# A deformable convolution's last stage: nine taps read where they lie, in 32-by-32 tiles of TensorE, for two row pairs at once

## The chip, the cores and the metric

The kernel runs on one core of a Trainium2 chip. The metric is device time in microseconds of one execution. The kernel before was timed three times; the profile is of one execution, taken by the hardware profiler, in which instructions of TensorE (PE, with its weight loads as PEld), VectorE (DVE), ScalarE (ACT), GpSimd (POOL) and SyncE (SP, which issues all DMAs of the main loop) have their start and duration.

## What is computed

Eight images of 32 channels, 128 by 128, fp32. Two blocks follow each other, each adding its result to its input after a normalization per channel:

```python
x = x + _L0_conv_ref(_gn(x), ...)      # spectral mix in x and y, plus a 1x1 channel mix
x = x + _L1_conv_ref(_gn(x), ...)      # deformable 3x3 convolution
# inside _L1_conv_ref: 27 offset/mask channels by a plain 3x3 convolution,
# nine samples per output pixel at shifted places, bilinear, times a sigmoid mask, then
out = jnp.einsum('bckhw,ock->bohw', vals, weight.reshape(Oc, -1, K2))   # the last stage
return out + bias[None, :, None, None]
```

The change is about the last einsum (nine taps `k`, 32 input channels `c`, 32 output channels `o`), the bias and the residual that is added behind it.

## The kernel before, in words

Four images make a group of 128 partitions (partition = 32 * image + channel); there are two groups. The first block and the second normalization end at about 285 us. Everything after that is the main loop, over 128 row pairs (two groups of 64). A row pair is 2 rows by 128 columns, 256 pixels for each of the 128 partitions.

Every engine runs the same software pipeline, `step(N, q, on, place)` with `q = N % 2`, in six rounds `r`. Step N computes, for different row pairs:

- for pair N: the offsets and masks (`OM`, line 983, round 0; their transposition, line 1005, round 1; then ACT, DVE and POOL make interpolation weights, lines 569 to 589, 739, 576, 579, 493);
- for pair N - 1: in each round POOL and ACT make products and their fp16 halves (lines 469, 559, 478), DVE transposes them (line 718), PE spreads them over the pixels of a region (`expand`, line 950, into the four PSUM banks of `pE`), and ACT and DVE each copy half of `pE` to SBUF (lines 565 and 731). In four of the rounds PE also transposes image strips (line 1016), which ACT copies (line 598);
- for pair N - 2: in each round the samples `V` (line 971), 2 or 3 column tiles times 4 images, into `pV`, copied to `VS[q]` by ACT (line 585), in round 3 by DVE (line 750). Here a partition is 32 * image + channel, and the nine taps lie beside each other in the free dimension;
- for pair N - 3: the last convolution. It contracts over 96 rows = 3 values of ky times 32 channels. For that, SP copies `VS` from one set of partitions to another through twelve DMAs per pair (line 405) into `v2`; in round 4 PE does 12 matmuls (line 996), DVE adds bias and residual `x1r` (line 758), and SP stores `outs` (line 392).

On PE the order within a step is: `expand` of the round, V of the round, then in round 0 OM, in round 4 the convolution, in round 1 the transposition of OM, and in rounds 1, 2, 3 and 5 the strip transposes. An fp32 matmul stands in the trace as two matmul records, each with its weight load; so 12 matmuls are 24 records. A transpose or an fp16 matmul is one record.

In the steps at the start, in the middle and at the end the code is written out (`peeled`); all others are a loop of two steps. The first steps have no convolution yet, since no pair has come so far.

## Time and profile before

| | us |
|---|---|
| median of 3 runs | 2406.02 (2404.01 to 2407.63) |
| the profiled execution, its own time | 2404.01 |
| its span, first to last instruction | 2402.0 |
| main loop, from about | 285 |

How to read it: the page first gives each engine's busy time. A second view, the timeline, shows instructions in the order of time, equal ones merged: start in us, busy us of the merged piece, engine, line, operation, what it writes and reads, its count, and in brackets the idle time of the engine ahead of it with the instruction that ended that. "issue" there is idle time that no other engine ended. A third view cuts the time into windows and gives the clock that was granted to TensorE in them (1.00 is 2.4 GHz, 0.50 is 1.2 GHz).

### The profile page before, as it was taken

To read this page: it belongs to the slowest core of one execution; us is meant where nothing else is said; L and a number is where in the kernel's file an instruction comes from. 1 tells how busy PE (TensorE), PEld (TensorE's weight loads), DVE (VectorE), ACT (ScalarE), POOL (GpSimd) and SP (SyncE) were. 2 spreads that over 40 slices of the span, in tenths; PEclk is the share of its full clock that TensorE was granted. 3 is DMA by queue.
4 is the path that set the end of the run, shared out by engine and by line. 5 is a ranking of instruction groups with operands and counts; after the bars stand their busy time and mean duration, and the time that the engine had idled before them with its cause. 6 is when DMAs were issued, how large, how long until landed. Compare 5 with 4: busy or idle time off the path is not lost.

```text
span 2402.0 us, 126528 instructions
## 1 busy us (share of the span) xinstructions
PE 2034.2 (85%) x50241; PEld 1359.9 (57%) x50241; DVE 1585.7 (66%) x2558; ACT 1787.6 (74%) x3238; POOL 1400.8 (58%) x1803
## 2 busy tenths in 40 slices
PE   8555188988988998898998899889889888988985
PEld 3311056666666666666666666666666666666663
DVE  8699066666666666666666666666666666666663
ACT  0003488888888888888888888888888888888884
POOL 0000166666666666666666666666666666666662
PEclk9699599999999999999999999999999999999997
DMA  8036545556555555655555555565555556556553
GB/s 311 1 140 271 200 115 154 147 149 156 143 149 150 147 151 148 156 143 150 152 147 151 151 154 147 148 156 144 148 152 146 150 148 155 145 149 154 145 151 87
DMA packets 196541, 363.81 MB, mean 151 GB/s; under 512 B 39760, under 2 KB 122480, under 8 KB 192368
## 3 DMA queue, kind: packets, MB, share of 16 engines
q1 hardware_dynamic: 196464, 362.74, 55.7%
q8 instruction: 54, 0.88, 0.2%
q14 instruction: 23, 0.19, 0.0%
HBM read 159.38 MB, written 52.22 MB: 88 GB/s over the span
## 4 chain that ended last, share of the span: by engine, by line
PE 29%; ACT 21%; issue 21%; SPq 5%; DVE 5%; POOL 2%; ACTq 1%; DVEq 1%; DMA 0%; POOLq 0%
PE pV L971 8%; PE pM L996 8%; ACT halves L559 7%; ACT big L585 5%; PE pE L950 5%; SPq L405 4%; PE pR L1016 4%; ACT big L576 4%; PE pM L983 4%; ACT big L598 3%; DVE big L731 2%; DVE big L718 1%; ACT msk L589 1%; POOL halves L478 1%; POOL prod L469 1%
## 5 line engine op out<-in xcount | busy, mean ns | idle before, releaser
L478 POOL TENSOR_TENSOR halves<-prod,halves 128x300 f16<-128x300 f32 x768 | 626.4, 816 | 377.2 <-ACT halves L559 377.1
L731 DVE COPY big<-pE 128x768 f32<-128x768 f32 x768 | 716.9, 933 | 191.3 <-PE pE L950 189.0
L971 PE MATMUL pV<-big 128*32 128x144 f32 x16384 | 816.9, 331 | 4.7 <-issue 1.4
L565 ACT ACTIVATE big<-pE 128x768 f32<-128x768 f32 x768 | 659.7, 859 | 107.7 <-PE pE L950 107.6
L469 POOL TENSOR_TENSOR prod<-big 128x300 f32<-128x300 f32 x768 | 554.2, 722 | 100.8 <-POOL big L493 32.2
L718 DVE STREAM_TRANSPOSE big<-halves 128x384 f32<-128x384 f32 x768 | 440.2, 573 | 197.2 <-POOL halves L478 193.4
L950 PE MATMUL pE<-big,sel_s 32*128 32x64 f16 (+1 forms) x24576 | 411.3, 203 | 174.8 <-DVE big L731 103.6
L950 PEld LDWEIGHTS pE<-big,sel_s 32*128 32x128 f16 x24576 | 329.6, 92 | 386.0 <-issue 373.4
L971 PEld LDWEIGHTS pV<-big 128*32 128x32 f32 x16384 | 482.2, 112 | 102.2 <-issue 6.7
L559 ACT ACTIVATE halves<-prod 128x300 f16<-128x300 f32 x768 | 484.3, 631 | 3.2 <-POOL prod L469 3.0
L493 POOL TENSOR_TENSOR big<-big,msk 128x360 f32<-128x360 f32 x128 | 107.2, 838 | 484.5 <-ACT big L579 484.5
L1016 PE MATMUL pR<-ident,strips 128*128 128x128 f32 x2048 | 330.2, 284 | 38.6 <-ACT big L598 38.6
L585 ACT ACTIVATE big<-pV 128x432 f32<-128x432 f32 (+1 forms) x640 | 315.0, 492 | 12.5 <-PE pV L971 12.5
L598 ACT ACTIVATE big<-pR 128x512 f32<-128x512 f32 x512 | 307.2, 600 | 20.1 <-PE pR L1016 3.1
L1016 PEld LDWEIGHTS pR<-ident,strips 128*128 128x128 f32 x2048 | 221.8, 141 | 161.5 <-ACT big L598 85.0
L739 DVE TENSOR_TENSOR big<-pM,cols_s 128x720 f32<-128x720 f32 x128 | 116.4, 909 | 219.6 <-ACT msk L589 219.6
L983 PE MATMUL pM<-big,wom 96*32 96x256 f32 x3072 | 193.7, 384 | 47.1 <-DMA big<-xh_scratch 47.1
L569 ACT ACTIVATE om_s<-pM,bom_s 128x256 f32<-128x256 f32 x128 | 61.4, 479 | 213.7 <-PE pM L983 213.7
L996 PE MATMUL pM<-v,wc 96*32 96x256 f32 x3072 | 203.7, 395 | 14.2 <-DMA v<-big 14.2
L983 PEld LDWEIGHTS pM<-big,wom 96*32 96x32 f32 x3072 | 99.8, 112 | 103.1 <-issue 50.6
L758 DVE SCALAR_TENSOR_TENSOR outs<-pM,bias_s,x1r 128x256 f32<-128x256 f32 x128 | 62.6, 489 | 128.8 <-PE pM L996 128.8
L996 PEld LDWEIGHTS pM<-v,wc 96*32 96x32 f32 x3072 | 103.5, 111 | 72.5 <-DMA v<-big 15.4
(72 smaller groups left out, 1175.1 us busy)
## 6 DMA issues: line engine op xcount, KB each, us to landing
v<-big SPq DMA_DIRECT2D x1536, 96.0 KB
win<-xh_scratch SPq DMA_DIRECT2D x128, 544.0 KB, 4.2
big<-xh_scratch SPq DMA_DIRECT2D x384, 136.0 KB, 4.1
xh_scratch<-win SPq DMA_DIRECT2D x32, 544.0 KB, 2.7
big<-in_x SPq DMA_DIRECT2D x16, 1024.0 KB, 16.4
x_scratch<-big SPq DMA_DIRECT2D x16, 1024.0 KB, 3.9
x1r<-x_scratch SPq DMA_DIRECT2D x128, 128.0 KB, 2.1
out<-outs SPq DMA_DIRECT2D x128, 128.0 KB, 1.8
```

Source lines behind the costliest of these rows:

```text
L469: nc.gpsimd.tensor_tensor(prod[:, rn % 2, :, :].rearrange("p m (a b) -> p m a b", a=NSH), hy.to_broadcast([P, RB, NSH, NSH]), hx.to_broadc ...
L478: nc.gpsimd.tensor_tensor(half[:, rn % 2, :, 0:SQ, 1], prod[:, rn % 2, :, :], half[:, rn % 2, :, 0:SQ, 0], ALU.subtract).then_inc(low_done, 1)
L559: nc.scalar.activation(half[:, rn % 2, :, 0:SQ, 0], prod[:, rn % 2, :, :], ACT.Copy).then_inc(high_done, 1)
L565: nc.scalar.activation(*expanded(1 - q, r, 0), ACT.Copy).then_inc(e_act, 1)
L585: nc.scalar.activation(*evacuate(q, r), ACT.Copy).then_inc(v_act, 1)
L718: nc.vector.transpose(PT[:, rn % 2, :], halves[:, rn % 2, :]) \
L731: nc.vector.tensor_copy(*expanded(1 - q, r, 1)).then_inc(e_dve, 1)
L950: last = mm(o, sel_s[part, (i + ky) * (KS + 1) + ox, :], rhs, start=(h == 0), stop=(h == 1))
L971: last = mm(pV[r % 2][b * C:(b + 1) * C, o:o + TAPC], XT[q][:, t * P + b * C:t * P + (b + 1) * C], av[:, b * NT + t, :, :], start=True, st ...
L983: last = mm(pM[b * C:(b + 1) * C, 0:PX], wom[:, kx, :], wino[0:KS * C, q, b, :, x0:x0 + W], start=(kx == 0), stop=(kx == KS - 1))
L996: last = mm(pM[b * C:(b + 1) * C, PX:2 * PX] .rearrange("p (i t j) -> p t i j", i=TILE_R, t=NT), wc[:, kx, :], v2[:, b, :, :].rearrange("p ...
L1016: last = nc.tensor.transpose(pR[:, u * P:(u + 1) * P], strips[:, t:t + 2, :, :].rearrange("p s r x -> p (s r x)"), ident[:, :])
```

## The change

The convolution is done once in two steps, at the head of every even step (`q == 0`, round 0), for the pairs N - 4 and N - 3, which lie in `VS[0]` and `VS[1]`. It reads `VS` in place: each matmul contracts over the 32 channels of one image, for one tap. There are 16 outputs, 4 images times 4 rows (2 pairs of 2 rows), each 32 output channels by 128 columns, in 16 different 32-by-32 tiles of the array (row of the tile from the image, column from the output row). Each output accumulates ten matmuls: nine taps, and one with the identity that brings the residual. So 160 matmuls (320 records with as many weight loads) for two pairs stand where 24 matmuls (48 records) stood. The results go to columns 384 to 511 of the four banks of `pE`. ACT copies two of the banks with the bias, DVE the other two. The twelve copies per pair between partitions, `v2` and DVE's line 758 are gone. The samples' layout in `VS` and in `pV` has all nine taps apart (`k=TAPS`), so the V matmul writes its output in runs of two elements.

```diff
-        wc = sb("wc", [KS * C, KS, C])
-        v2 = sb("v2", [KS * C, IPG, KS, PX])
+        wc = sb("wc", [P, TAPS, C])
...
+        pC = pE[:, :].rearrange("p (a n) -> p a n", a=QUADS)[:, :, RPX:RPX + W]
...
-            dst = VS[q].rearrange("p (k t n) -> p t k n", k=KS, t=NT)[:, tiles[0]:tiles[0] + n]
-            return dst, pV[gi % 2][:, 0:n * TAPC].rearrange("p (t k n) -> p t k n", t=n, k=KS)
+            dst = VS[q].rearrange("p (k t n) -> p t k n", k=TAPS, t=NT)[:, tiles[0]:tiles[0] + n]
+            return dst, pV[gi % 2][:, 0:n * TAPC].rearrange("p (t k n) -> p t k n", t=n, k=TAPS)
...
+                sp.dma_start(wc[r, :, :], wct.rearrange("k c o -> c k o")).then_inc(blocks_ld, 16)
...
-                if on[3]:
+                if on[3] and q == 0:
+                    g, local = place(N - 4)
+                    sp.wait_ge(out_act, N - 2)
+                    sp.wait_ge(out_dve, N - 2)
+                    rows = out[g * P:(g + 1) * P, bass.ds(local * PX, 2 * PX)] \
+                        .rearrange("(b o) (r x) -> r o b x", b=IPG, x=W)
+                    for k in range(2 * TILE_R):
+                        sp.dma_start(rows[k], outs[k * C:(k + 1) * C, :, :]).then_inc(out_st, 16)
+                if on[2] and q == 1:
                     g, local = place(N - 3)
-                    for b in range(IPG):
-                        for ky in range(KS):
-                            sp.dma_start(v2[ky * C:(ky + 1) * C, b, :, :].rearrange("c k n -> c (k n)"),
-                                         VS[q][b * C:(b + 1) * C, ky * KS * PX:(ky + 1) * KS * PX]) \
-                                .then_inc(v2_ld, 16)
+                    wait(sp, conv_done, N - 3)
+                    sp.dma_start(x1r[:, :], x1_d[g * P:(g + 1) * P, bass.ds(local * PX, 2 * PX)]).then_inc(x1_ld, 16)
...
+                    if on[3] and q == 0 and r == 0:
+                        act.wait_ge(conv_done, N - 2)
+                        wait(act, out_st, (N - 4) * 32)
+                        nc.scalar.activation(outs[:, 0:2, :], pC[:, 0:2, :], ACT.Identity,
+                                             bias=bias_s[:, 0:1]).then_inc(out_act, 2)
...
+                    if on[3] and q == 0 and r == 0:
+                        dve.wait_ge(conv_done, N - 2)
+                        wait(dve, out_st, (N - 4) * 32)
+                        nc.vector.tensor_scalar(outs[:, 2:4, :], pC[:, 2:4, :], bias_s[:, 0:1], None,
+                                                ALU.add).then_inc(out_dve, 2)
...
-                    if on[3] and r == CONV_AT:
-                        n = N - 3
-                        dve.wait_ge(conv_done, n + 1)
...
-                        nc.vector.scalar_tensor_tensor(out=outs[:, 1 - q, :], in0=pM[:, PX:2 * PX],
-                                                       scalar=bias_s[:, 0:1], in1=x1r[:, 1 - q, :],
-                                                       op0=ALU.add, op1=ALU.add).then_inc(out_ready, 1)
...
+                    if on[3] and q == 0 and r == 0:
+                        pe.wait_ge(e_act, min(N - 1, PAIRS) * ROUNDS if isinstance(N, int) else (N - 1) * ROUNDS)
+                        pe.wait_ge(e_dve, min(N - 1, PAIRS) * ROUNDS if isinstance(N, int) else (N - 1) * ROUNDS)
+                        pe.wait_ge(v_act, (N - 2) * VN[1])
+                        pe.wait_ge(v_dve, (N - 2) * VN[0])
+                        pe.wait_ge(x1_ld, N * 8 - 16)
...
+                        for k in range(TAPS + 1):
+                            kx, ky = divmod(k, KS)
+                            for b, d, i in itertools.product(range(IPG), range(2), range(TILE_R)):
+                                c, row = slice(b * C, (b + 1) * C), d * TILE_R + i
+                                if k < TAPS:
+                                    w, rhs = wc[c, ky * KS + kx, :], VS[d][c, k * PX:(k + 1) * PX] \
+                                        .rearrange("p (t i x) -> p i t x", t=NT, i=TILE_R)[:, i]
+                                else:
+                                    w, rhs = ident[c, c], x1r[c, row * W:(row + 1) * W].rearrange("p (t x) -> p t x", t=NT)
+                                last = mm(pC[row * C:(row + 1) * C, b, :].rearrange("p (t x) -> p t x", t=NT), w, rhs,
+                                          start=(k == 0), stop=(k == TAPS))
+                        last.then_inc(conv_done, 2)
                     if on[1]:
+                        if on[3] and q == 0 and r == 1:
+                            pe.wait_ge(out_act, N - 2)
+                            pe.wait_ge(out_dve, N - 2)
                         expand(N - 1, r)
...
-                                last = mm(pV[r % 2][b * C:(b + 1) * C, o:o + TAPC],
+                                last = mm(pV[r % 2][b * C:(b + 1) * C, o:o + TAPC]
+                                          .rearrange("p (k m j) -> p m k j", k=KS, j=2),
                                           XT[q][:, t * P + b * C:t * P + (b + 1) * C],
-                                          av[:, b * NT + t, :, :], start=True, stop=True)
+                                          av[:, b * NT + t, :, :, :], start=True, stop=True)
...
-                    if on[3] and r == CONV_AT:
-                        n = N - 3
-                        pe.wait_ge(v2_ld, (n + 1) * (16 * NV2))
...
-                        for kx in range(KS):
-                            for b in range(IPG):
-                                last = mm(pM[b * C:(b + 1) * C, PX:2 * PX]
-                                          .rearrange("p (i t j) -> p t i j", i=TILE_R, t=NT), wc[:, kx, :],
-                                          v2[:, b, :, :].rearrange("p k n -> p (k n)")
-                                          .rearrange("p (m k j) -> p m k j", k=KS, j=2)[:, :, kx, :],
-                                          start=(kx == 0), stop=(kx == KS - 1))
-                        last.then_inc(conv_done, 1)
```

## Rows read from the trace of the kernel before

**Rows 1.** The page's first part: engine, busy us, share of span, instructions
```profile
PE 2034.2 (85%) x50241; PEld 1359.9 (57%) x50241; DVE 1585.7 (66%) x2558; ACT 1787.6 (74%) x3238; POOL 1400.8 (58%) x1803
```
**Rows 2.** Windows: us, busy per engine (count), granted clock, DMA share, GB/s
```profile
1295.00:1425.00 130.00, 117.00 (x3103) 81.12 (x3096) 85.72 (x128) 108.31 (x200) 86.27 (x111) 1.00 0.60 154
1100.00:1230.00 130.00, 117.03 (x3108) 80.38 (x3107) 86.71 (x129) 109.39 (x202) 87.82 (x113) 1.00 0.58 151
```
**Rows 3.** Timeline of one step of the loop, from round 4 to OM
```profile
1214.09 0.53 PE L950 MATMUL pE<-big,sel_s 32*128 32x64 f16 x32 [0.50 <-issue]
1215.21 1.58 PE L996 MATMUL pM<-v,wc 96*32 96x256 f32 x24
1215.24 0.92 DVE L731 COPY big<-pE 128x768 f32<-128x768 f32 x1
1216.71 0.53 PE L950 MATMUL pE<-big,sel_s 32*128 32x64 f16 x32
1217.00 0.48 DVE L758 SCALAR_TENSOR_TENSOR outs<-pM,bias_s,x1r 128x256 f32<-128x256 f32 x1 [0.84 <-PE pM L996]
1217.96 0.66 PE L1016 MATMUL pR<-ident,strips 128*128 128x128 f32 x4
1218.09 0.41 ACT L585 ACTIVATE big<-pV 128x288 f32<-128x288 f32 x1
1218.96 0.54 PE L950 MATMUL pE<-big,sel_s 32*128 32x64 f16 x32 [0.35 <-DVE big L731]
1219.51 1.17 PE L971 MATMUL pV<-big 128*32 128x144 f32 x24
1220.50 1.48 PE L983 MATMUL pM<-big,wom 96*32 96x256 f32 x24
1221.91 0.53 PE L950 MATMUL pE<-big,sel_s 32*128 32x64 f16 x32
1222.13 0.48 ACT L569 ACTIVATE om_s<-pM,bom_s 128x256 f32<-128x256 f32 x1 [1.60 <-PE pM L983]
```
**Rows 4.** Timeline, PE alone, of an early step that has no convolution
```profile
323.94 0.54 PE L950 MATMUL pE<-big,sel_s 32*128 32x64 f16 x32 [0.51 <-issue]
...
326.05 0.54 PE L950 MATMUL pE<-big,sel_s 32*128 32x64 f16 x32 [0.80 <-DVE big L731]
...
327.29 0.66 PE L1016 MATMUL pR<-ident,strips 128*128 128x128 f32 x4
...
328.84 1.17 PE L971 MATMUL pV<-big 128*32 128x144 f32 x24 [0.43 <-ACT big L598]
329.79 1.52 PE L983 MATMUL pM<-big,wom 96*32 96x256 f32 x24
```
**Rows 5.** Groups by line: shapes, count, busy us, mean ns of one record, idle before
```profile
L950 PE MATMUL pE<-big,sel_s 32*128 32x64 f16 (+1 forms) x24576 | 411.3, 203 | 174.8 <-DVE big L731 103.6 <-issue 62.8 <-DVE big L718 7.6
L983 PE MATMUL pM<-big,wom 96*32 96x256 f32 x3072 | 193.7, 384 | 47.1 <-DMA big<-xh_scratch 47.1
L996 PE MATMUL pM<-v,wc 96*32 96x256 f32 x3072 | 203.7, 395 | 14.2 <-DMA v<-big 14.2
```
**Rows 6.** DMA queues, window 1290 to 1430, then window 500 to 1290: packets, MB, share
```profile
q8 instruction: 24, 0.39, 1.2%
...
q8 instruction: 1, 0.02, 0.0%
```
**Rows 7.** Timeline of the end of the span
```profile
2374.50 0.41 ACT L585 ACTIVATE big<-pV 128x288 f32<-128x288 f32 x1 [1.08 <-PE pV L971]
...
2382.71 7.74 SPq L405 DMA_DIRECT2D v<-big  x12
2392.09 2.79 PE L996 MATMUL pM<-v,wc 96*32 96x256 f32 x24 [9.88 <-DMA v<-big]
...
2394.95 0.48 DVE L758 SCALAR_TENSOR_TENSOR outs<-pM,bias_s,x1r 128x256 f32<-128x256 f32 x1 [13.14 <-PE pM L996]
```

More of the change, by code:

```diff
@@ L47 @@
 TAPC = TAPS * TILE_R * TILE_C
-OM_AT, OMT_AT, CONV_AT = 0, 1, 4
+OM_AT, OMT_AT = 0, 1
 T_AT = (1, 2, 3, 5)
@@ L224, in build @@
         wino_ld = [sem(f"wino_ld{i}") for i in range(2)]
-        v2_ld = sem("v2_ld")
-        x1_ld = [sem(f"x1_ld{i}") for i in range(2)]
-        out_st = [sem(f"out_st{i}") for i in range(2)]
+        x1_ld = sem("x1_ld")
+        out_st = sem("out_st")
         om_done = sem("om_done")
@@ L388, in step @@
                     load_window(N + 1, 1 - q, place)
-                if on[3]:
-                    g, local = place(N - 3)
-                    sp.wait_ge(out_ready, N - 2)
-                    sp.dma_start(out[g * P:(g + 1) * P, bass.ds(local * PX, PX)], outs[:, 1 - q, :]) \
-                        .then_inc(out_st[1 - q], 16)
-                if on[1]:
-                    g, local = place(N - 1)
-                    wait(sp, out_ready, N - 2)
-                    sp.dma_start(x1r[:, 1 - q, :], x1_d[g * P:(g + 1) * P, bass.ds(local * PX, PX)]) \
-                        .then_inc(x1_ld[1 - q], 16)
-                if on[2]:
-                    sp.wait_ge(v_act, (N - 1) * VN[1])
-                    sp.wait_ge(v_dve, (N - 1) * VN[0])
-                    wait(sp, conv_done, N - 2)
-                    for b in range(IPG):
-                        for ky in range(KS):
-                            sp.dma_start(v2[ky * C:(ky + 1) * C, b, :, :].rearrange("c k n -> c (k n)"),
-                                         VS[q][b * C:(b + 1) * C, ky * KS * PX:(ky + 1) * KS * PX]) \
-                                .then_inc(v2_ld, 16)
+                if on[3] and q == 0:
[7 more added lines that the diff above has]
+                if on[2] and q == 1:
+                    g, local = place(N - 3)
+                    wait(sp, conv_done, N - 3)
+                    sp.dma_start(x1r[:, :], x1_d[g * P:(g + 1) * P, bass.ds(local * PX, 2 * PX)]).then_inc(x1_ld, 16)
             steps(sp, step)
-            for q in range(2):
-                sp.wait_ge(out_st[q], 16 * (NPAIR // 2) * g_count)
+            sp.wait_ge(out_st, 64 * (NPAIR // 2) * g_count)
             sp.wait_ge(flag_set, 1)
@@ L582, in step @@
                         act.wait_ge(v_done, (N - 2) * len(VGROUPS) + (r + 1))
-                        if v_count(1, r) == 0:
-                            wait(act, v2_ld, (N - 3) * (16 * NV2))
+                        if v_count(1, r) == 0 and q == 0:
+                            wait(act, conv_done, N - 2)
                         nc.scalar.activation(*evacuate(q, r), ACT.Copy).then_inc(v_act, 1)
@@ L747, in step @@
                         dve.wait_ge(v_done, (N - 2) * len(VGROUPS) + (r + 1))
-                        if v_count(0, r) == 0:
-                            wait(dve, v2_ld, (N - 3) * (16 * NV2))
+                        if v_count(0, r) == 0 and q == 0:
+                            wait(dve, conv_done, N - 2)
                         nc.vector.tensor_copy(*evacuate(q, r)).then_inc(v_dve, 1)
-                    if on[3] and r == CONV_AT:
-                        n = N - 3
-                        dve.wait_ge(conv_done, n + 1)
-                        dve.wait_ge(x1_ld[1 - q], (n - (1 - q)) * 8 + 16)
-                        m = (n - (1 - q)) * 8
-                        if not (isinstance(m, int) and m == 0):
-                            dve.wait_ge(out_st[1 - q], m)
-                        nc.vector.scalar_tensor_tensor(out=outs[:, 1 - q, :], in0=pM[:, PX:2 * PX],
-                                                       scalar=bias_s[:, 0:1], in1=x1r[:, 1 - q, :],
-                                                       op0=ALU.add, op1=ALU.add).then_inc(out_ready, 1)
             steps(dve, step)
@@ L977, in step @@
                         wait(pe, msk_done, N)
-                        wait(pe, out_ready, N - 3)
                         pe.wait_ge(wino_ld[q], (N - q) * (8 * KS) + 16 * KS)
```

23 lines of the change are left out of this document (11 added, 12 removed).

## The prediction

> **What bounds the kernel now.** I read the page's busy times first [rows 1]: PE is busy for 85% of the span, ACT for 74%, DVE for 66%. In the main loop PE is busy for 117.0 of 130 us at a granted clock of 1.00, the full 2.4 GHz [rows 2]. So PE is nearly the bound, but no engine is full, and what a piece of work is worth must be read from the order of one step. I took the timeline of a step [rows 3], where the reader is to follow PE: E4 (`expand` of round 4) starts at 1214.09, the convolution at 1215.21, E5 at 1216.71, strip transposes at 1217.96, E0 at 1218.96, V0 at 1219.51, OM at 1220.50. From OM a chain of offsets, masks and weights runs through ACT, DVE and POOL to E4 and E5 of the same step, with ACT nearly without a gap. From E4 to the next OM is 6.41 us, and the time of a step is the chain from OM to E4 plus these 6.41. There were 8 steps in 130 us, 16.2 us each [rows 2].
>
> The trace has one stretch of the same six pieces without a convolution, in an early step [rows 4]: E4 at 323.94, E5 at 326.05, OM at 329.79, so 5.85 us. It is the best witness of what removing the convolution brings: 0.56 us, not the 1.50 us that PE gives it. The reader is to see why: E5 there waits 0.80 us for DVE's copy (line 731), which before lay under the convolution (it runs from 1215.24 to 1216.16 in rows 3), and V0 waits 0.43 us for ACT.
>
> **Part by part.**
>
> *Removed, each step:* 24 records on PE, 1.50 us, and DVE's line 758, 0.48 us with its wait of 0.84 us [rows 3]. By the early step both together are worth 0.56 us of a step [rows 3, 4]. The twelve copies per pair end no wait in the loop: the row of the old convolution has no idle time ahead of it [rows 3], and of its 14.2 us of waiting for the copies [rows 5] 9.88 stand ahead of the very last convolution [rows 7]. I price them at nothing in the loop.
>
> *Added, every second step:* 320 records on PE at the head of the step, between the transposes and E0. Call their time T. The trace has no 32-by-32 fp32 tiles running beside each other, so I bound T.
> - Below: OM is six rounds of four tiles, 256 columns; (1.48 - 0.38) / 5 = 0.22 us a round [rows 3, 5], 0.11 us for 128 columns. If all 16 tiles run together there are 20 rounds, 2.2 us.
> - From V: 24 records in 1220.50 - 1219.51 = 0.99 us, six rounds of 0.165 us for 144 columns [rows 3]. Four tiles with weights of their own do not get below this. 20 rounds make 3.3 us.
> - From `expand`, the only piece with 32-row tiles beside each other: (0.53 - 0.20) / 31 = 10.6 ns per record [rows 3, 5]. 320 records make 3.4 us. For 2.2 us a record would have to follow every 6.9 ns, which no row here shows over a whole piece.
> - Above: if only two tile rows of the four run together, 6.6 us; one after the other, 13.2 us (4 x 3.3). `expand` has four tile rows at once, so I give these little.
>
> I take 3.3 us, since two rows of different kind meet there.
>
> The Trainium skill, TensorE: Matmul & The Clock Gate, section "The mechanism", says that tiles of a packed group start about 4 ns apart and then run together; by that rule T would be the lower bound, 2.2 us, and this is the first rival below. No row here shows 4 ns.
>
> *What waits behind it.* The convolution stands ahead of E0 and waits for both copies of E5 and for the last V copy. In the early step the copy of E5 by DVE starts with the end of E5; in rows 3 the last V copy by ACT ends at 1218.50, 1.79 us after E5, the latest of them. So it starts 1.85 us after E5. Then T, 0.1 us to drain (OM: 1221.91 - 1220.50 = 1.41 = 6 x 0.22 + 0.09), about 0.5 us from E0 to V0 and 0.97 us to OM. E4 to OM: 2.11 + 1.85 + T + 0.1 + 0.5 + 0.97 = T + 5.53, against 6.41. Behind the waiting PE stands everything: E0, V0, OM and the chain.
>
> *Sum for two steps:* even step T - 0.88, odd step -0.56, together T - 1.44. With T = 3.3 it is +1.86 us. There are 62 such couples (N = 4 to 126): +115 us.
>
> *Moved to ACT and DVE, every second step:* one copy of 256 elements each, like line 569 (0.48 us) and line 758 (0.48 us). They stand behind the first copies of `expand`, while PE does V0 and OM: E1 comes 2.95 us after E0, ACT's first copy and this one are through after about 0.6 + 0.9 (as line 731) + 0.5 = 2.0 us, and ACT then still waits for OM (1.60 us idle in rows 3). Nothing. If V0 and OM were shorter by 1 us it would cost 0.1 us.
>
> *Access patterns.* V now writes PSUM in runs of two. The nearest row is the old convolution (runs of two read, of eight written) against OM, same columns: 1.50 against 1.41 us, 7% per round [rows 3]. On 32 rounds of 0.165 us that would be 0.37 us a step, +46 us over 126 steps; below, nothing. V reads in runs of two already and gets only 144 columns into 0.165 us, so there is room for the writes: I take 0. The Trainium skill, PSUM — Partial Sum Buffer, section "Specifications (TRN2)", says that any non-contiguous pattern slows matmuls significantly and gives no figure; it speaks for the upper end. The V copies of ACT and DVE write in runs of 16 elements instead of 48; 0.
>
> *SP:* twelve DMA issues fewer per pair, four stores of half the size instead of two, one load instead of two, each with a step of slack: 0. *Start:* the weights of the convolution are loaded in more, smaller pieces, under the second group's image load: 0.
>
> *End of the span.* Before, the last V copy but one ends at 2374.91, then come the copies (7.74 us of issue), a convolution at half clock (2.79 us) and line 758 at 2394.95 [rows 7]. Now the last V group and its copy follow at once (about 1.0 us), then T: 2374.9 + 1.0 + 3.3 = 2379.2, the rest as before. That is -15.8; the convolution at N = 128 costs T - 0.3 = +3.0. Together -13 us.
>
> Span 2402.0 + 115 - 13 = 2504, and 2 us around it (2404.01 against 2402.0) make **2506**. The profiled execution lies 2 us under the median; I leave that.
>
> **The rivals.**
>
> *The tiles run fully together* (T = 2.2). Two steps cost 0.76 us: +47, end -14: 2402 + 33 + 2 = 2437. For it: OM's rounds show no loss with four tiles. Against: V's rounds do. 0.24.
>
> *Something slows PE further.* (a) V's output pattern, +46 us on 2506: 2552. (b) Two tile rows at a time: T = 6.6, 62 x 5.16 = 320, end -10: 2714. (c) Code. In the 8 written-out steps 24 packets of instructions arrive, in 790 us of loop one [rows 6]; so the loop of two steps, some six packets, stays on the chip. It grows from 1552 to 2096 matmul and load records, over eight packets. Should it no longer fit, the fetches come in each turn. The written-out steps, with busy PE 117.00 against 117.03 us, say that costs nothing [rows 2]. But the convolution eats 2.5 packets in 3.3 us, and a packet takes 1.1 us (1.2% of 16 engines over 140 us, over 24); if each is waited for, +2.75 us, 62 times: 2676. The Trainium skill, Advanced Engine Details and Errata, section "ISA Cache", gives TensorE 128 KB, which the new loop would pass and the old one not. Together 0.20 beyond the forecast's own bounds.
>
> *Faster: the freed time comes back whole.* The early step is one step, with pipelines just filling; if the chain of other engines follows PE, removing gives g = 1.5 us per step instead of 0.56. Two steps then cost T - 0.32 - 2g. With T = 2.2: -1.12 x 62 - 14: 2321. With T = 3.3: 2390. It is faster from g = 0.83 (T = 2.2) or g = 1.39 (T = 3.3) upwards. Against: the 0.80 us wait for DVE ahead of E5. 0.10.
>
> *The change does not do what it says:* the tiles serialize altogether, T = 13.2: 62 x 11.76 = 729, end -3: 3130. 0.03.
>
> **How the numbers follow.** The forecast (T from 2.9 to 3.9 us, with up to half of the pattern's cost) has 0.43 and reaches from 2480 to 2565. The range reaches down to the fast tiles and up into the slowed cases: 2430 to 2640; outside are the faster case (0.10) and about 0.09 above. A measurement of this kernel can tell about 0.2% from no change. Faster 0.10, within 0.2% 0.02, slower 0.88.
>
> **What would show it.** The 320 records as one piece of 3.3 us between transposes and E0 of every second step, PE idle about 0.8 us before E5 on DVE, odd steps near 15.6 us and even ones near 18.6 us, V0 to OM still at 0.99 us; ACT idle under the convolution; the end 13 us shorter. Wrong it is if the piece takes 2.2 or over 4 us, if V0 to OM grows, if instruction packets come in the loop, or if odd steps shrink by over 1 us.

## The result, and the profile after

| | before | after |
|---|---|---|
| median of the runs, us | 2405.02 (2399.09 to 2407.63) | 3315.62 (3311.06 to 3317.82) |
| span of the profiled execution, us | 2402.0 | 3311.2 |
| granted clock, mean | 0.97 | 0.83 |
| packets of instructions | 54 | 630 |

The ratio is 1.379 (1.376 to 1.382). I had said 2506, in a range up to 2640. The direction was right; the size was about nine times too small.

The page of the kernel after, first the busy times as in [rows 1], then its queue of instruction packets (packets, MB, share), then three groups of its fifth part (count | busy, mean ns | idle before, releaser):

```profile
PE 2463.6 (74%) x67649; PEld 1662.3 (50%) x67649; DVE 1564.5 (47%) x2494; ACT 1812.7 (55%) x3302; POOL 1387.4 (42%) x1803
...
q8 instruction: 630, 10.32, 1.3%
...
L727 DVE COPY big<-pE 128x768 f32<-128x768 f32 x768 | 718.1, 935 | 1167.7 <-PE pE L941 1166.7
...
L556 ACT ACTIVATE big<-pE 128x768 f32<-128x768 f32 x768 | 648.7, 845 | 919.1 <-PE pE L941 918.8
...
L964 PE MATMUL pE<-big,wc 32*32 32x128 f32 x18432 | 419.2, 396 | 371.9 <-issue 371.4
```

The reader is to see four things. ACT and DVE do as much as before, and their copies of `pE` wait some 900 to 1200 us for PE (108 and 191 us before). PE's own share fell from 85% to 74%, so PE is not full of work either. And ahead of the new convolution (line 964) PE stood idle for 371 us with "issue" as the releaser: no semaphore that the profile shows held it. And there are 12 times as many packets of instructions.

The step times below are the distances between ACT's copies of OM, one for each step. Before they are 16.1 to 16.3 us in both loops. After, the odd steps take 15.6 to 16.3 (median 16.1 in the first loop, 15.6 in the second). The even ones take 30 to 33 in the loops (median 31.4 and 32.1) and 27.0 to 29.2 in the written-out steps between them and in the first turn of the second loop.

The timeline of PE in an even step of the loop, with E0, V0, OM and E1 of it, and ahead of it V0 and OM of the odd step:

```profile
1601.49 1.17 PE L986 MATMUL pV<-big 128*32 128x144 f32 x24 [0.30 <-ACT big L594]
1602.48 1.48 PE L998 MATMUL pM<-big,wom 96*32 96x256 f32 x24
...
1614.42 0.53 PE L941 MATMUL pE<-big,sel_s 32*128 32x64 f16 x32 [0.74 <-DVE big L727]
...
1615.66 0.66 PE L1016 MATMUL pR<-ident,strips 128*128 128x128 f32 x4
1620.16 2.05 PE L964 MATMUL pE<-big,wc 32*32 32x128 f32 x83 [3.84 <-issue]
1622.64 2.81 PE L964 MATMUL pE<-big,wc 32*32 32x128 f32 x128 [0.44 <-issue]
1626.93 1.79 PE L964 MATMUL pE<-big,wc 32*32 32x128 f32 x73 [1.49 <-issue]
...
1629.52 0.61 PE L941 MATMUL pE<-big,sel_s 32*128 32x64 f16 x18
...
1630.91 1.67 PE L986 MATMUL pV<-big 128*32 128x144 f32 x24
1632.35 2.79 PE L998 MATMUL pM<-big,wom 96*32 96x256 f32 x24
1635.07 0.83 PE L941 MATMUL pE<-big,sel_s 32*128 32x64 f16 x32
```

The same in a written-out even step, between the two loops:

```profile
1755.71 0.66 PE L1016 MATMUL pR<-ident,strips 128*128 128x128 f32 x4
1756.46 1.82 PE L964 MATMUL pE<-big,wc 32*32 32x128 f32 x120
1760.33 1.90 PE L964 MATMUL pE<-big,wc 32*32 32x128 f32 x128 [2.04 <-issue]
1765.45 1.11 PE L964 MATMUL pE<-big,wc 32*32 32x128 f32 x37 [3.21 <-issue]
...
1767.35 0.83 PE L941 MATMUL pE<-big,sel_s 32*128 32x64 f16 x32
```

The pieces are the key. The convolution breaks into runs, and a whole run is 128 matmuls with 128 weight loads. A packet has 10.32 MB / 630 = 16.4 KB; over the 256 instructions of a whole run that is 64 bytes each. That these packets are PE's own code can be seen in [rows 6]: 24 came there for eight steps of new code, and eight steps have 4 x 1552 = 6208 matmul and load records of PE, 24.3 packets. So each run is one packet of code: PE eats one in 1.9 us, and the next run starts 5.1 us after it (1760.33 to 1765.45). In the written-out step nothing waits ahead of the first run; in the loop there are 3.84 us more in front of it.

How many packets come, in both stretches of the kernel after (windows as in [rows 2], then the queue in the same window):

```profile
500.00:1600.00 1100.00, 851.85 (x24344) 588.34 (x24334) 494.49 (x725) 646.58 (x1192) 504.44 (x654) 0.83 0.21 55
...
q8 instruction: 232, 3.80, 1.5%
...
1744.00:1874.00 130.00, 102.32 (x3148) 71.95 (x3144) 64.20 (x93) 82.56 (x153) 64.86 (x85) 0.89 0.23 61
...
q8 instruction: 25, 0.41, 1.3%
```

Written out: 130 / 25 = 5.2 us for a packet. In the loop: 1100 / 232 = 4.7 us. Both are averages over stretches in which PE waits for code only part of the time. Two steps have 2096 matmul and load records, 8.2 packets, and took 43.3 us on average where they are written out. That 8.2 x 5.2 gives nearly the same is bookkeeping, since written-out code is fetched once; it doesn't show a limit. The odd step has 2.8 packets, one per 5.5 us, and does not wait. The limit shows where PE stands: within the convolution the trace has the packets 3.3 to 5.7 us apart, in the middle 3.9, while each carries 1.9 us of work. In the loop a turn takes 47.6 us, 10.0 packets, about two more than it holds.

### The profile page after: what moved, and what is told of

It reads as the page before. It is cut to its first block and busy times, and to the rows that moved or that the text cites. A ratio compares the mean times of both kernels' runs of the same rounds, so it can differ in the third digit from the quotient of the medians.

```text
span 3311.2 us, 159684 instructions
## 1 busy us (share of the span) xinstructions
PE 2463.6 (74%) x67649; PEld 1662.3 (50%) x67649; DVE 1564.5 (47%) x2494; ACT 1812.7 (55%) x3302; POOL 1387.4 (42%) x1803
## 3 DMA queue, kind: packets, MB, share of 16 engines
q8 instruction: 630, 10.32, 1.3%
## 5 line engine op out<-in xcount | busy, mean ns | idle before, releaser
L469 POOL TENSOR_TENSOR halves<-prod,halves 128x300 f16<-128x300 f32 x768 | 611.7, 797 | 1312.2 <-ACT halves L550 1312.1
L986 PE MATMUL pV<-big 128*32 128x144 f32 x16384 | 856.3, 342 | 23.2 <-ACT big L594 20.0
L964 PE MATMUL pE<-big,wc 32*32 32x128 f32 x18432 | 419.2, 396 | 371.9 <-issue 371.4
L941 PE MATMUL pE<-big,sel_s 32*128 32x64 f16 (+1 forms) x24576 | 454.0, 211 | 250.5 <-DVE big L727 159.3
L941 PEld LDWEIGHTS pE<-big,sel_s 32*128 32x128 f16 x24576 | 357.4, 96 | 485.7 <-issue 296.7
L986 PEld LDWEIGHTS pV<-big 128*32 128x32 f32 x16384 | 501.2, 117 | 136.5 <-issue 34.9
L964 PEld LDWEIGHTS pE<-big,wc 32*32 32x32 f32 x18432 | 306.4, 131 | 471.3 <-issue 438.8
L594 ACT ACTIVATE big<-pR 128x512 f32<-128x512 f32 x512 | 307.2, 600 | 27.4 <-PE pR L1016 10.3
L581 ACT ACTIVATE big<-pV 128x432 f32<-128x432 f32 (+1 forms) x640 | 310.0, 484 | 11.4 <-PE pV L986 10.9
L998 PE MATMUL pM<-big,wom 96*32 96x256 f32 x3072 | 258.7, 484 | 46.7 <-DMA big<-xh_scratch 46.7
L998 PEld LDWEIGHTS pM<-big,wom 96*32 96x32 f32 x3072 | 122.2, 140 | 135.2 <-issue 99.8
L476 POOL COPY strips<-win 128x1088 f32<-128x1088 f32 x128 | 139.5, 1090 | 0.0
## 6 DMA issues: line engine op xcount, KB each, us to landing
big<-in_x SPq DMA_DIRECT2D x16, 1024.0 KB, 16.3
```

Source lines behind the costliest of these rows:

```text
L469: nc.gpsimd.tensor_tensor(half[:, rn % 2, :, 0:SQ, 1], prod[:, rn % 2, :, :], half[:, rn % 2, :, 0:SQ, 0], ALU.subtract).then_inc(low_done, 1)
L581: nc.scalar.activation(*evacuate(q, r), ACT.Copy).then_inc(v_act, 1)
L941: last = mm(o, sel_s[part, (i + ky) * (KS + 1) + ox, :], rhs, start=(h == 0), stop=(h == 1))
L964: last = mm(pC[row * C:(row + 1) * C, b, :].rearrange("p (t x) -> p t x", t=NT), w, rhs, start=(k == 0), stop=(k == TAPS))
L986: last = mm(pV[r % 2][b * C:(b + 1) * C, o:o + TAPC] .rearrange("p (k m j) -> p m k j", k=KS, j=2), XT[q][:, t * P + b * C:t * P + (b + 1) ...
L998: last = mm(pM[b * C:(b + 1) * C, 0:PX], wom[:, kx, :], wino[0:KS * C, q, b, :, x0:x0 + W], start=(kx == 0), stop=(kx == KS - 1))
```

## The experiments

**Theory A**: the loop's code no longer stays on the chip, and PE waits for it, once behind each jump back and again within the convolution. **Theory B**: the work itself is slow (16 small tiles, weight loads, patterns). Where an expectation has further theories, it names them.

### The kernel before with a loop of four steps

```diff
-UNROLL = 2
+UNROLL = 4
```

> The kernel before with its main loop made four steps long instead of two; every engine does the same work in the same order, only the loop's body is twice as long (about 3100 matmul and weight-load records of TensorE against 1552). Theory A (code): a body that does not fit on the chip is fetched anew in each turn. Then q8 shows some 12 packets per turn, about 3 per step, in the whole loop. The written-out steps of before took 16.2 us with 3 packets per step, so this should cost little in this kernel: 0 to 3%, 2405 to 2480 us. Theory B (the 16-tile piece itself is slow, code plays no part): the same time, and it would also be so under A if fetches at 3 packets per 16 us are always early; the packets tell whether the body is held.

Measured: 2650.9 us, ratio 1.103 (1.101 to 1.105), with 456 packets. The body is fetched in each turn, as Theory A said, but at 10% instead of 0 to 3%: the expectation had priced code by the written-out steps again and left out the jump. The old convolution, no small tile in it. One step of four, the one behind the jump, takes 23 to 24 us (median of each loop), the others mostly 16.2 to 17.5. Its queue from 700 to 1200 us, and PE behind a jump:

```profile
q8 instruction: 97, 1.59, 1.4%
```

```profile
847.59 0.66 PE L1016 MATMUL pR<-ident,strips 128*128 128x128 f32 x4
851.04 0.53 PE L950 MATMUL pE<-big,sel_s 32*128 32x64 f16 x32 [2.79 <-issue]
851.61 1.34 PE L971 MATMUL pV<-big 128*32 128x144 f32 x24
852.71 0.63 PE L983 MATMUL pM<-big,wom 96*32 96x256 f32 x1
853.82 2.78 PE L983 MATMUL pM<-big,wom 96*32 96x256 f32 x23 [0.48 <-issue]
```

What follows: a body that is not held costs 7 to 8 us behind the jump even in the old kernel, by waiting 2.8 us behind the jump, by more waits after it, and by the clock, since OM takes 2.78 us instead of 1.48. A packet comes every 500 / 97 = 5.2 us. A turn of 73 us takes 14 of them and holds 3104 / 256 = 12.1; again about two too many. What the two are, whether code fetched past the jump and thrown away, no row tells. The three steps without a jump ask for a packet per 5.4 us and cost 0 to 1.3 us more than 16.2: that is code just fast enough.

### The kernel after with fewer blocks in the convolution

```diff
-                        for k in range(TAPS + 1):
+                        for k in (*range(3), TAPS):
```

> The changed kernel with the convolution cut to taps 0, 1 and 2 and the residual: 4 of its 10 blocks of 16 matmuls (the other six taps are left out of the output). Records of TensorE in the loop's body: 1712 against 2096. Theory A (code, the body fits on the chip): no instruction packets in the loop, even steps of about 16.2 - 0.88 + 0.4 x 3.3 = 16.6 us, odd ones 15.6, in all about 2385 us. Theory B (16 tiles are slow in themselves, 13 us for ten blocks): the piece takes 4 x 1.3 = 5.2 us, even steps 20.5 us, about 2630 us.

> The changed kernel with 7 of the 10 blocks (taps 0 to 5 and the residual; three taps are left out of the output). Records in the loop's body: 1904. Theory A (code): the edge lies between 1552 records, which are held, and 2096, which are not. If 1904 fit, even steps take 16.2 - 0.88 + 0.7 x 3.3 = 17.6 us, 2450 us in all; if they do not, over 22 us and over 2700 us, with packets in the loop. Theory B: 7 x 1.3 = 9.1 us, even steps 24.4 us, about 2880 us, and on a straight line between 4 and 10 blocks.

The run with seven blocks has `range(6)` in that place.

Measured: 2814.2 us with four blocks (436 packets), 3119.5 with seven (590 packets). Neither theory had 2814: with four blocks the body was expected to stay on the chip, and it did so in part alone. With seven, the even steps take 28.5 in the loop and 24.2 to 25.8 written out. With four, in the first loop they alternate between 17.7 and 25; in the second all take about 26; written out 18.9 to 20.8. Odd steps take 15.6 to 16.3 in both, with two exceptions among the written-out ones of four blocks (18.8 and 16.7). The couples N = 64 to 69 (two of them written out, the third a first turn) had no jump ahead: on average 36.1 us for 6.7 packets, 40.7 for 7.4, and 43.3 for the 8.2 of the kernel after. The time of two steps rises with the number of their instructions, by 4.6 and 2.7 us for equal additions, so not as a fixed price for each. Where four blocks left the even step its 17.7 us, two packets came in it, and five in the one of 25.

### The expansion halved, so that the whole convolution fits

```diff
-                    for h, u in itertools.product(range(2), range(QUADS)):
+                    for h, u in itertools.product(range(1), range(QUADS)):
-                        last = mm(o, sel_s[...], rhs, start=(h == 0), stop=(h == 1))
+                        last = mm(o, sel_s[...], rhs, start=True, stop=True)
```

> The changed kernel with all 10 blocks of the convolution, but with the spreading matmuls (expand) of the high fp16 halves alone: 192 matmuls and as many loads fewer in the loop's body, 1712 records, as many as with 4 blocks. The low halves are left out, so the samples are less exact. Theory A (code): no packets in the loop, the convolution in 3 to 4 us at the full clock, even steps about 18 us; in all 2450 to 2520 us, less what the shorter expand gives. Theory B: the convolution still takes 13 us, over 3200 us.

> The kernel before with the spreading matmuls of the high fp16 halves alone (the low halves are left out, as in a_half_expand). It is the partner of a_half_expand, in whose first group the loop ran without instruction packets at 17.6 + 19.9 = 37.5 us for two steps. Theory A (even with its code on the chip the new convolution costs more than the two old ones, since its piece takes 4.3 us there): 15.3 to 16.0 us a step, 31 to 32 us for two, so the new form is 5 to 6 us slower per couple. Rival (only code is to blame): 18.7 us a step, 37.5 for two.

Measured: the kernel after 2868.7 us with 202 packets, where 2450 to 2520 was expected since the body was to be held throughout; the kernel before 2358.1, with steps of 15.7 and 16.0 as expected. The body has 1712 records with its 320 for the convolution. In the first loop it is held from the twelfth step on; the queue from 500 to 1250 us:

```profile
q8 instruction: 1, 0.02, 0.0%
```

There the steps take 19.9 and 17.6 us, 37.5 for two, where the kernel before with the same cut takes 31.7. In the second loop nearly every other turn has most of the packets and takes 15.4 + 31.2; the one after it has few and takes 15.4 + 19.9. It is the same code and the same work in one execution, so 11.3 us of an even step are the fetching of code, with the clock that falls while PE waits. For these 11.3 us the comparison leaves no room for Theory B: small tiles, patterns and order are the same in both turns. What the held couple costs over the 31.7 of before, 5.8 us, is the work's own. PE of a held stretch, the even step and then the end of the odd one:

```profile
663.81 3.87 PE L964 MATMUL pE<-big,wc 32*32 32x128 f32 x281 [0.49 <-issue]
...
668.13 0.35 PE L941 MATMUL pE<-big,sel_s 32*128 32x64 f16 x16
668.56 1.17 PE L986 MATMUL pV<-big 128*32 128x144 f32 x24
...
681.57 0.51 PE L941 MATMUL pE<-big,sel_s 32*128 32x64 f16 x16 [1.16 <-DVE big L727]
...
685.00 1.67 PE L986 MATMUL pV<-big 128*32 128x144 f32 x24 [0.32 <-ACT big L594]
686.44 2.32 PE L998 MATMUL pM<-big,wom 96*32 96x256 f32 x24
```

The convolution is one run now, 668.13 - 663.81 = 4.32 us, 13.5 ns a record, with the code at hand and V0 at its full-clock 1.17 us. That is T of the prediction, and it is 4.3, not 3.3. In the odd step the granted clock falls near 681.3, after 6 us in which PE was busy for 3.74: E5 0.51 us instead of 0.36, V0 1.67, OM 2.32.

### The loop turned by one step

```diff
-            peeled(0, 4)
+            peeled(0, 5)
-                first, loops = g * NPAIR + 4, (NPAIR - 5) // UNROLL
+                first, loops = g * NPAIR + 5, (NPAIR - 6) // UNROLL
-                        step(j * UNROLL + (first + q), q % 2, [True] * 4,
+                        step(j * UNROLL + (first + q), (q + 1) % 2, [True] * 4,
```

> The changed kernel with its loop turned by one step: the body begins with the odd step, so the jump back falls between an even and an odd step and no longer right ahead of the convolution. All work and its order are the same. Theory A (two costs of code: a wait behind each jump back, 7 us in b_loop4, and packets eaten faster than they come within the convolution): the 3.8 us of idle time ahead of the convolution go, even steps fall from 31.5 to about 27 us, as in the written-out steps, and odd ones rise from 15.6 to 20 to 23 us; in all about the same, 3250 to 3450 us. Rival (the wait ahead of the convolution is a drain or a semaphore of its own): even steps stay at 31.5, odd ones at 15.6.

Measured: 3405.0 us. The jump now stands ahead of the odd step, which takes 22.7 us in the first loop and 20.5 in the second (medians) instead of 16.1 and 15.6; the even one takes 27.4 to 27.6 (26.5 to 28.9) instead of 31.4 to 32.1, as the written-out even steps of the kernel after. The odd step behind the jump:

```profile
1627.40 0.66 PE L1016 MATMUL pR<-ident,strips 128*128 128x128 f32 x4
1631.88 0.56 PE L941 MATMUL pE<-big,sel_s 32*128 32x64 f16 x32 [3.83 <-issue]
1634.74 1.67 PE L986 MATMUL pV<-big 128*32 128x144 f32 x24 [2.30 <-issue]
```

The 3.84 us ahead of the convolution moved with the jump, to work that has nothing to do with it. So the two costs are apart: 4 to 5 us behind a jump that stands ahead of the even step (4.8 to 6.5 ahead of the odd one), and the wait within the convolution.

### The kernel after with a loop of four steps

The edit is that of the first experiment.

> The changed kernel with four steps written out in its loop instead of two, so that half as many jumps back are taken; every operation of the step is the same. Theory A (a turn pays once for the jump, about 4 to 5 us of wait ahead of the convolution, and each convolution pays by itself about 11 us because its instructions come too slowly): the even step behind a jump stays at 31 to 32 us, the other even step of the turn costs what the written-out steps of the changed kernel cost, 27 to 28 us; with some 28 fewer jumps at 4.3 us the time falls by about 120 us, to 3190 (3150 to 3240). Theory B (the surplus is the work itself: small tiles, their order, the output pattern): where the jumps are changes nothing, 3300 to 3330. Theory C (a body of twice the size is worse in every step): over 3330.

Measured: 3196.5 us (Theory A had 3190), 575 packets. Even steps 31 behind the jump, the others 27 to 29, odd ones 15.6 to 16.3. Half the jumps are gone, and the steps without a jump ahead take what the written-out ones take. The same edit costs the kernel before 10% and brings the kernel after 4%: once the code isn't held anyway, a longer body has fewer turns to pay for.

### What a held record costs

All three runs here have the halved expansion too, so that there are stretches whose code is held.

```diff
-                            for b, d, i in itertools.product(range(IPG), range(2), range(TILE_R)):
+                            for d, i, b in itertools.product(range(2), range(TILE_R), range(IPG)):
```

> a_half_expand with the 16 matmuls of a block in another order: image (tile row) fastest, so that neighbours in the queue lie in different tile rows; before it was output row (tile column) fastest. Theory A (the 13.5 ns per record come from starts in one tile row that follow each other): in the stretches whose code is held the piece falls from 4.3 us towards 3.4 us, 10.6 ns per record. Rival (the array or the queue is full at that rate whatever the order): 4.2 to 4.4 us. Slower than 4.4 us would say that alternating rows hurts.

Measured: 2882.1 us; the piece takes 4.33 us, the steps 17.6 and 19.9. Which tile follows which makes no difference.

```diff
-    w, rhs = wc[c, ky * KS + kx, :], VS[d][c, k * PX:(k + 1) * PX] \
-        .rearrange("p (t i x) -> p i t x", t=NT, i=TILE_R)[:, i]
+    w, rhs = wc[c, ky * KS + kx, :], VS[d][c, k * PX + i * W:k * PX + (i + 1) * W] \
+        .rearrange("p (t x) -> p t x", t=NT)
```

> The changed kernel with the expansion from the high halves alone, as in a_half_expand, and with the convolution's samples read as 128 elements in a row instead of 16 runs of 8 (each matmul then reads other samples than the convolution wants; count, shapes and tiles of the matmuls are the same). It tells whether the 4.3 us of the held convolution (13.5 ns for each of 320 records, against the 10.6 ns of my sum) come from reading in runs of 8. If so: the piece takes 3.3 to 3.6 us where the code is held, and the time falls by some 0.8 us in each of about 40 held couples and more where the clock then holds, 2790 to 2850. If not: the piece stays at 4.2 to 4.4 us, its steps at 17.6 and 19.9 us, the time at 2860 to 2890.

Measured: 2866.1 us, 3.87 us for the same 281 records, steps of 17.6 and 19.9. Reading in runs of eight costs nothing here.

```diff
+    t = slice(0, NT // 2) if 0 < k < TAPS else slice(0, NT)
-    last = mm(pC[row * C:(row + 1) * C, b, :].rearrange("p (t x) -> p t x", t=NT), w, rhs,
+    last = mm(pC[row * C:(row + 1) * C, b, :].rearrange("p (t x) -> p t x", t=NT)[:, t], w, rhs[:, t],
```

> The changed kernel with the expansion from the high halves alone, as in a_half_expand, and in the convolution the eight taps 1 to 8 take 64 of their 128 columns (the other half of their sums is left out); tap 0 and the residual keep all 128, so the piece still has 320 matmuls with a weight load each, but 16384 columns by 16 tiles fall to 64 x 128 + 256 x 64. It tells what the 13.5 ns per record of the held convolution are made of. If columns (the tiles share the array's time by columns): 4.3 us fall to 4.3 x 0.6 = 2.6 us, even held steps to about 18.3 us. If each matmul with its load has a floor of its own (an issue or load cost near 10.6 to 13.5 ns): the piece stays at 3.4 to 4.3 us, held steps at 19.0 to 19.9. The steps without held code, 26 to 31 us, are the same in both, since they wait for as many instructions.

Measured: 2844.0 us. A held even step, PE alone:

```profile
492.25 3.07 PE L965 MATMUL pE<-big,wc 32*32 32x128 f32 x284 [0.53 <-issue]
...
495.73 0.35 PE L941 MATMUL pE<-big,sel_s 32*128 32x64 f16 x16
...
497.13 1.49 PE L999 MATMUL pM<-big,wom 96*32 96x256 f32 x24
```

The piece takes 495.73 - 492.25 = 3.48 us, 0.84 less than 4.32, for 256 halved records: 3.3 ns each, from 13.5 to 10.2 ns (which takes the other 64 as unchanged). Columns alone would have given 6.8. So both views held in part. A record of 64 columns costs 10.2 ns, close to the 10.6 ns of `expand`, whose records have 64 columns too; one of 128 costs 13.5. My sum had put the price of a 64-column record on one of 128. The held steps were mostly 15.4 and 19.1 us, 34.5 together: 3.0 less than in a_half_expand, of which 0.84 is the piece and 2.2 the odd step, where the clock did not fall.

### Versions of the kernel before

The timeline showed [rows 3] that E5's copy by DVE can wait behind line 758 and that E4 to E5 hangs on the convolution between them. I moved line 758 a round later, and a third of the convolution (kx of 0) a round earlier:

```diff
-                    if on[3] and r == CONV_AT:
+                    if on[3] and r == ROUNDS - 1:
                         n = N - 3
                         dve.wait_ge(conv_done, n + 1)
...
-                    if on[3] and r == CONV_AT:
+                    if on[3] and r in (CONV_AT - 1, CONV_AT):
...
-                        for kx in range(KS):
+                        for kx in (range(1) if r < CONV_AT else range(1, KS)):
...
-                        last.then_inc(conv_done, 1)
+                        if r == CONV_AT:
+                            last.then_inc(conv_done, 1)
```

The other three versions take one part of this edit or shift it, as their expectations say.

> The kernel before with its old convolution in two parts: the four matmuls of kx = 0 in round 3 behind V, where TensorE then waits for ACT, the eight of kx = 1 and 2 in round 4 as before, and DVE's line 758 in round 5 behind its copy of expand instead of ahead of its transpose. Same work in all. Theory (what the convolution costs is what does not fit under DVE's copy ahead of E5, 0.56 us a step by the early step): 0.2 to 0.45 us a step come back, 126 times, 2350 to 2385 us. Rival (the chain through ACT sets the step, V0 waits for it anyway): under 0.1 us a step, 2395 to 2406 us.

> The kernel before with one edit: VectorE's addition of the convolution's result (its line 758) is done one round later, and the convolution stays whole where it was. In b_split this was done together with moving a third of the convolution a round earlier, and its steps took 15.7 us instead of 16.2, yet its written-out stretches took 18 to 20 us, with 8.6 us of waits for V's transfers ahead of the convolution in 90 us. If the gain came from VectorE (E's copy of the next round had waited behind the addition): steps of 15.8 to 16.0, written-out stretches as before, 2360 to 2392. If it came from the split: within 0.3% of the kernel before, 2398 to 2412.

> The kernel before with two thirds of the convolution (kx of 0 and 1) a round earlier and the last third where it was, and VectorE's addition one round later. If the split gives the gain by putting PE work where PE had waited for E's copies: steps of 15.6 to 15.8 as in b_split; the written-out stretches wait for V's transfers as in b_split, so 2380 to 2400. If a longer piece in the earlier round takes that away: steps of 16.0 to 16.3, 2400 to 2440.

> The kernel before with VectorE's addition one round later everywhere, and a third of the convolution (kx of 0) a round earlier in the loop's steps alone; the written-out steps keep the convolution whole. b_split's loop steps took 15.6 and 15.8 us and its written-out ones 18 to 20; b_dve_late's took 16.0 and 16.1, and its written-out ones 16.1. If the slow written-out steps of b_split come from the earlier third there (V's transfers not landed): loop steps 15.7, written-out ones 16.2, about 22 us below b_split: 2360 to 2372. If they come from something else in the written-out code: 2385 to 2395 as b_split.

| version | us | ratio to before | loop steps | written-out steps between the loops |
|---|---|---|---|---|
| line 758 later alone (b_dve_late) | 2393.3 | 0.995 (0.993 to 0.997) | 16.0, 16.1 | 16.1 to 18.5 |
| and kx of 0 earlier (b_split) | 2389.1 | 0.994 (0.992 to 0.996) | 15.6, 15.8 | 16.5 to 20.2 |
| kx of 0 and 1 earlier (b_split2) | 2434.9 | 1.012 (1.010 to 1.014) | 16.1, 16.3 | 17.2 to 19.9 |
| kx of 0 earlier in the loop alone (b_split_in_loop) | 2367.5 | 0.985 (0.984 to 0.987) | 15.6, 15.8 | 16.1 to 17.5 |

The old convolution's row in the written-out stretch 1295 to 1425, of the kernel before, of b_split and of b_split_in_loop:

```profile
L996 PE MATMUL pM<-v,wc 96*32 96x256 f32 x192 | 12.6, 391 | 0.0
```

```profile
L996 PE MATMUL pM<-v,wc 96*32 96x256 f32 x172 | 16.7, 500 | 14.4 <-DMA v<-big 14.4
```

```profile
L996 PE MATMUL pM<-v,wc 96*32 96x256 f32 x192 | 13.3, 391 | 4.7 <-DMA v<-big 4.7
```

Asked for a round earlier, V's copies between partitions had not landed there, and PE stood 14.4 us instead of 4.7, with a mean record of 500 ns against 391 since the clock fell too (granted 0.92 in this stretch). Kept whole there, the convolution still waits 4.7 us where the kernel before and b_dve_late have 0.0 in this window, and 22 us came back. Line 758 gives about 0.1 us of a step, the split another 0.3. b_split (2350 to 2385, or 2395 to 2406) and b_dve_late came out between their two cases, the other two in the range of one. Why two thirds in the earlier round give nothing stays open. The last version beats both kernels: 2367.5 us, 1.5% under the kernel before.

## Why the prediction was wrong, point by point

*The copies and the convolution removed.* Right. Odd steps came at 15.6 us as forecast in the second loop and at 16.1 in the first (why the first has more stays open), and the freed queues brought no more. The wait ahead of the convolution, 1.85 us after E5 by the sum, was 2.0 us where no jump stands ahead.

*V's output in runs of two.* Right at 0: V0 to OM is 0.99 us after as before (1601.49 to 1602.48). The Trainium skill's statement that any non-contiguous pattern slows matmuls significantly (PSUM — Partial Sum Buffer, "Specifications (TRN2)") is not borne out for this one.

*T.* Too small by 1.0 us: 4.32 where 3.3 stood, measured where the code is held. Two rows had met at 3.3 by chance; neither had 128 columns with 32-row tiles beside each other. With 4.3 the formula T - 1.44 gives +2.9 for two steps. a_half_expand and b_half_expand differ by 5.8; 2.2 of the rest are the clock in the odd step, 0.7 is left over. So even held, the change would cost some 5.8 x 62 = 360 us by these two runs, an estimate with half an expansion: 2760. T and the clock alone would have put the time past my range.

*The tiles' start.* By the Trainium skill (TensorE: Matmul & The Clock Gate, "The mechanism") tiles start about 4 ns apart; no held piece here got below 10.2 ns a record.

*Code: the step that failed.* The forecast's sum has no term for code: the prediction held that the written-out steps "say that costs nothing". It saw the mechanism and priced it in rival (c) at 1.1 us for a packet, 2.75 us for a convolution. 1.1 us was the time that a packet's bytes occupy the DMA engines. What counts is how often one comes while PE waits: every 3.9 us in the middle. From the convolution's first record to E0 it is 9.1 us in the first loop, 11.6 in the second and 10.9 written out (medians), against 3.4 in the sum. Half of it was in hand. In [rows 6] are 24 packets in 140 us, of which the steps with new code (six written out, and the first turn of the second loop) are 130: one per 5.4 us, while PE ate one per 5.4 us (2 x 16.2 us for 1552 records, 6.1 packets). That these steps cost nothing showed that 5.4 us is slow enough, and nothing of any faster rate; I read it as a bound on the cost of code, where it was a bound on the rate from one side. Had I taken 5.4 as the upper end of what a packet can cost, a couple would have had up to 8.2 x 5.4 = 44 us against the forecast's 34.3, +10 us in each of 62: rival (c) at up to 3120. That this comes near the written-out 43.3 is partly luck, since odd steps do not wait for code and a packet that PE waits for comes sooner than 5.4 us.

*The jump.* Not in the prediction at all. Behind each jump back the first packets are late (3.84 us ahead of the convolution), and each turn takes about two packets more than it holds. That makes 47.6 us instead of 43.3.

*The clock.* Not in the prediction either. PE idle for code goes on at 1.2 GHz: V0 1.67 us and OM 2.79 against 1.17 and 1.48 [rows 3]; the granted clock in the loop is 0.83. From E0 to ACT's copy of OM the even step takes 4.9 to 5.8 us (medians) where it took 3.2 before: 1.7 to 2.6 us a couple, the smaller part.

*The end of the span.* -10 us where -15.8 stood. From the end of the last V copy but one to the end of the last addition there were 20.5 us before [rows 7]; now it is 10.5, of which the convolution has 8.7 (3295.31 to 3304.01) because its packets come one by one there too:

```profile
3295.31 2.68 PE L964 MATMUL pE<-big,wc 32*32 32x128 f32 x186 [0.77 <-issue]
3299.62 1.56 PE L964 MATMUL pE<-big,wc 32*32 32x128 f32 x102 [1.63 <-issue]
...
3303.36 0.65 PE L964 MATMUL pE<-x1r,ident 32*32 32x128 f32 x6 [1.84 <-issue]
...
3304.12 0.48 DVE L731 TENSOR_SCALAR outs<-pE,bias_s 128x256 f32<-128x256 f32 x1 [10.49 <-PE pE L964]
```

*The rivals' ends.* By the sum's own formula the end of the span is -15 us for T = 2.2, -6 for 6.6 and +7 for 13.2, where the rivals have -14, -10 and -3. It moves them by 1 to 10 us and no chance hangs on it.

*The sum again.* In an even step all that is new lies between E5 and OM (medians, us; the rest of the step is 10.3 to 10.4 where it was 10.8):

| | forecast | written out | first loop | second loop |
|---|---|---|---|---|
| E5 to the convolution | 1.85 | 2.0 | 5.9 | 5.5 |
| convolution to E0 | 3.4 | 10.9 | 9.1 | 11.6 |
| E0 to ACT's copy of OM | 3.2 | 5.1 | 5.8 | 4.9 |

The first row has the jump, the second the wait for code and T, the third the clock. Of the 62 couples 56 lie behind a jump back: 47.6 - 32.4 = 15.2 us each make 850. Six do not (four written out, two the first turns of a loop): 43.3 - 32.4 = 10.9 each make 65. The steps ahead of them are 2 us shorter, all behind the last OM is 4 us shorter (+6 with the convolution at N = 128, -10 at the end), where the forecast had -13. Together 909, the 909.2 by which the spans differ.

## What to carry to other kernels

Count the instructions of a loop body before you trade wide matmuls for small ones: a body that outgrows what the chip holds is fetched in every turn. It then pays behind each jump back, and wherever the engine gets through its instructions faster than they come; a stretch of many short instructions runs at the speed of its code, whatever the work in it. The number for it stands in the profile: in a written-out stretch of the same kernel the packets per microsecond tell what rate is surely had, and a stretch that eats them faster is priced at up to that rate, not at the share of the DMA engines that the packets take. A price for a small tile is taken from a row with the same count of columns, or kept as a bound.

## What was not expected of the hardware

- A packet of 16.4 KB, 256 instructions of PE, came every 3.3 to 5.8 us while PE waited within a convolution (medians 3.9 to 4.6 in four kernels whose code is not held), against 1.9 us in which PE ran 128 matmuls with their loads. Little was there ahead of need: in the written-out step PE ran 120 matmuls and then stood (1756.46 to 1760.33).
- After a jump back in a body that isn't held, about two packets more than the body were fetched in each turn (10.0 for 8.2; 14 for 12.1), and the first wait behind the jump was 2.8 to 3.8 us.
- A body of 1552 records was always held, one of 1904 or more never. Two kernels have 1712: a_half_expand was held from the twelfth step on in the first loop and mostly every other turn in the second, a_blocks4 every other turn in the first and never in the second. So the count of records alone does not tell. The Trainium skill gives TensorE 128 KB (Advanced Engine Details and Errata, "ISA Cache"); at 64 bytes a record 1712 are 110 KB and 1904 are 122 KB, without the waits and branches, which are no records. So the edge found here lies somewhat below that figure, unless the waits and branches fill the rest. Why one loop holds a body that the other does not was not tried.
- 16 fp32 tiles of 32 by 32 with 128 columns and a weight load each cost 13.5 ns a record in either order of tiles and with either pattern of reading, with 64 columns 10.2 ns.
